# A relational graph layer on one core: five sweeps of neighbour sums instead of four, their groups spread evenly from unit 111

## The chip, the cores and the metric

The kernel runs on one core of a Trainium2 chip. The metric is device time in microseconds (us) of one execution; lower is better. TensorE is called PE here, VectorE DVE, ScalarE ACT, GpSimd POOL and SyncE SP.

## What is computed

```
h = relu(layernorm(x))                      # x: 1250 x 1024, fp32
u = h @ root + bias
for r in range(8):                          # 8 relations, 20000 edges, sorted by dst
    mask  = (edge_type == r)
    sums  = segment_sum(h[src] * mask, dst) # 1250 rows
    cnt   = segment_sum(mask, dst)
    u    += (sums / max(cnt, 1)) @ weight[r]
z   = concat([u, h]) @ w_gate + b_gate
out = x + tanh(u) * z + h * (1 - z)
```

All matrices are 1024 x 1024 in fp32, `w_gate` is 2048 x 1024.

## The kernel before

**Products.** The kernel multiplies first and sums afterwards: for each relation, y = h @ weight[r] goes to DRAM as two fp16 halves per value (`y_rows`, 4 KB a row), and the mean over a node's edges is taken of rows of y. PE's products run as eleven "gemms" in the order rel0, rel1, root, rel2 to rel7, gate_h, gate_u, cut into 325 **units**. A unit of the first three and of gate_u is 24 matmuls of 128 x 512; a unit of the other seven, which are done by a Winograd-like scheme of seven phases of five units, is 12 matmuls. `FIRST` gives each gemm's first unit: 0, 20, 40, 60, 95, 130, 165, 200, 235, 270, 305. Products go to four PSUM banks in turn, so PE may be four units ahead of what DVE and ACT have read out.

**Sums.** The edges are sorted into 80 **groups** (relation r, 125 destination rows j), each of some 250 edges, and a group's edges into **tiles** of 128, two or three a group. POOL prepares a tile: it copies its indices (L600), gathers 128 rows of y with an indirect DMA into a ring of four slots (L610; 4 KB a row), and makes a 128 x 125 one-hot matrix of the destinations (L618). It makes the one-hot of tile t-2 before it gathers tile t, so two gathers are in flight. PE multiplies one-hot and rows (L1243, four matmuls, and one for the counts, L1246) into PSUM banks 4 to 6. When the group's last tile is done, DVE divides by the counts and adds to the rows of u (L1111 to L1113, `add_group`). A tile's slot is free again when PE has done it; the next group's first tile waits for `add_group` of the group before, since banks 4 to 6 are the only ones.

**Sweeps.** u is too large to stay on chip, so the groups are walked in **sweeps** over the ten row blocks: sweep 0 has relations 0 to 2, sweep 1 has 3 and 4, sweep 2 has 5 and 6, sweep 3 has 7. In each, SP loads a block of 125 rows of u, the groups (j, r) of the sweep are added, and SP stores it again (L400, L409; three buffers). This is a **step**; a sweep has ten. A sweep's tiles are padded to a multiple of four; that gives 72, 48, 48 and 24 tiles with these edges, 192 in all. At a sweep's end POOL makes the last two one-hots, loads the next bounds, and waits until all rows of y of the next sweep's relations are stored (L635 to L646).

**Order.** All order is written by unit number. `AGG_AT[g]` is the unit behind which PE does the first tile of group g (`sum_first`), `REST_AT[g]` the unit behind which it does its other tiles (`sum_rest`). DVE does `add_group(g)` at the head of unit `REST_AT[g] + 1`. SP stores and loads a block of u two units after a step's last rest, ahead of that unit's y store in its queue. The list of edges is made on POOL with 160 indirect DMAs (L585) and comes back as a table, from which `table()` on DVE (L990 to L992) makes the indices at unit `TABLE_AT`, at the end of the unit's work.

In sweep 2 the first tile and the rest of a group stand at the same unit; in the other sweeps the rest is one unit later where the next group leaves room. The last groups, of rel7, are tied to the end of rel7's products (unit 269), and their results to gate_u, whose left operand is u.

Of the kernel before, what the change touches and what calls it, by code (L numbers as in the profile page):

```python
# [21 lines left out]
def gated_rgcn_preln(nc, x, src, dst, edge_type, weight, root, bias, w_gate, b_gate, out):  # L22
# [6 lines left out]
    NJ = N // DT  # L29
    NG = R * NJ  # L30
    RING = 4
    TMAX = 332
    HC = 512
    HT = 5
    KH = 4
# [2 lines left out]
    PAD = LT[NJ - 1][1]  # L38


    SWEEPS = [(0, 3), (3, 5), (5, 7), (7, 8)]
    NS = len(SWEEPS)
    SPAN = [(r0 * NJ, r1 * NJ) for r0, r1 in SWEEPS]
    assert EP * EC == E and NJ * DT == N and 2 * NG + E // P + NS * (RING - 1) <= TMAX - RING and TMAX % RING == 0
    assert len(LT) == NJ and D == 2 * KH * P and R == 8 and NJ == 2 * HT

    def group(g):

        for s, (a, b) in enumerate(SPAN):
            if g < b:  # L50
                r0, r1 = SWEEPS[s]
                j, r = divmod(g - a, r1 - r0)
                return s, j, r0 + r
# [60 lines left out]
    for n in range(NU):  # L114
# [4 lines left out]
        else:  # L119
# [2 lines left out]
            FREED.append((kind, tally[kind]))  # L122


    AGG_AT = ([98 + g * 67 // 30 for g in range(30)] + [168 + g * 68 // 20 for g in range(20)]
              + [238 + g * 34 // 20 for g in range(20)] + [273 + g * 28 // 10 for g in range(10)])
    assert all(AGG_AT[g] >= FIRST[W_OF[SWEEPS[group(g)[0]][1] - 1] + 1] + 3 for g in range(NG)) and AGG_AT == sorted(AGG_AT)

    REST_AT = [AGG_AT[g] + (1 if g + 1 < NG and AGG_AT[g + 1] >= AGG_AT[g] + 2 and group(g)[0] != 2 else 0) for g in range(NG)]
    AGG, REST = {}, {}  # L130
    for g in range(NG):
        AGG.setdefault(AGG_AT[g], []).append(g)
        REST.setdefault(REST_AT[g], []).append(g)
    STEPS = [(s, j) for s in range(NS) for j in range(NJ)]
    STEP_END = [REST_AT[SPAN[s][0] + (j + 1) * (SWEEPS[s][1] - SWEEPS[s][0]) - 1] for s, j in STEPS]
    FINAL = (NS - 1) * NJ
# [16 lines left out]
    SQ = 4  # L153
    KEYS_AT, SCAN_AT, TOTALS_AT, BOUNDS_AT = 2, {5: 0, 9: 1, 13: 2, 15: 3}, 17, 19
    POSITIONS_AT = {21: 0, 25: 1, 29: 2, 33: 3}
    TABLE_AT = AGG_AT[0] - 3
    NCONST = 5 + 2 * NS

    hs_rows = nc.dram_tensor("hs_rows", [N, D], F32).ap()
    y_rows = [nc.dram_tensor(f"y_rows{i}", [(r1 - r0) * N, 2 * D], F16).ap() for i, (r0, r1) in enumerate(SWEEPS)]  # L160
    table_rows = nc.dram_tensor("table_rows", [P * TMAX, 1], I32).ap()
    zh_rows = nc.dram_tensor("zh_rows", [N, D], F32).ap()
# [62 lines left out]
    with ctx:  # L225
        def sb(name, shape, dt):
            return ctx.enter_context(nc.sbuf_tensor(name, shape, dt))
# [9 lines left out]
        early = sb("early", [P, 8 * D], F32)  # L237
        edges = sb("edges", [P, TMAX, 2], I32)
        table_i = sb("table_i", [P, TMAX], I32)
        tb = sb("tb", [P, NG], F32)  # L240
# [118 lines left out]
        def _(sp):  # L359
# [73 lines left out]
            for n in range(NU):  # L433
# [35 lines left out]
                if n == FIRST[W_ROOT + 1] + 2:  # L469
                    sp.wait_ge(s[YDONE], 2 * NJ * (W_ROOT + 1))  # L470
                    load_brow(b_gate)
                if n == AGG_AT[0] - 2:
                    for b in range(4):
# [47 lines left out]
        def _(pool):  # L521
# [112 lines left out]
            for i in range(NS):  # L634
                q0 = pool.value_load(turns[0:1, i:i + 1], min_val=0, max_val=TMAX // RING - 2)  # L635
                q1 = pool.value_load(turns[0:1, i + 1:i + 2], min_val=0, max_val=TMAX // RING - 1)
                for b in range(4):
# [160 lines left out]
        def _(dve):  # L798
# [356 lines left out]
            for n in range(NU):  # L1155
# [28 lines left out]
                if n in POSITIONS_AT:  # L1184
                    positions(POSITIONS_AT[n])
                if n == TABLE_AT:
                    table()
# [13 lines left out]
        def _(pe):  # L1201
# [127 lines left out]
            for n in range(NU):  # L1329
# [12 lines left out]
                for g in range(NG):  # L1342
                    if AGG_AT[g] == n:
                        sum_first(g)
                    if REST_AT[g] == n:
                        sum_rest(g)
# [26 lines left out]
```

## Time and profile before

| | us |
|---|---|
| median of 3 runs | 1476.33 |
| lowest, highest | 1475.23, 1481.91 |
| the profiled execution | 1475.66 |
| its span in the trace | 1473.8 |
| PE busy in the span | 1294.7 (88%) |
| DVE busy | 938.9 (64%) |
| POOL busy | 728.8 (49%) |
| ACT busy | 409.2 (28%) |
| moved by DMA | 259.15 MB, 176 GB/s over the span |

The span is the time from the first to the last instruction of the trace. PE is the busiest engine but stands still for parts of the span. The products of the units are line L1285, those of the tiles L1243. Units can be found in the trace by counting: each is 12 (or 24) matmuls of L1285. A timeline row with "x60" is five units of 12.

### The profile page before, as it was taken

Reading aid. Unit: us, or ns where it says so; the run is one execution under the profiler, and the core shown is the slowest. Engines: PE = TensorE matmul, PEld = TensorE weight load, DVE = VectorE, ACT = ScalarE, POOL = GpSimd, SP = SyncE. Lnnn points to the kernel's source line nnn. Section 1 sums busy time; section 2 is a strip of 40 time slices with the busy share of each in tenths; the row PEclk is TensorE's granted clock in tenths of the full one; section 3 lists DMA queues with packets and bytes.
Section 4 is the critical chain, followed back from the end, with each engine's and each line's share of the span. In section 5 each row is a group of like instructions: output and inputs, shape, how many; then the busy total and the mean of one; then the engine's idle time right before and its main releaser. Section 6 shows DMA issues by size and latency. Waiting matters only on the chain.

```text
span 1473.8 us, 19899 instructions
## 1 busy us (share of the span) xinstructions
PE 1294.7 (88%) x6165; PEld 650.2 (44%) x6165; DVE 938.9 (64%) x1256; ACT 409.2 (28%) x501; POOL 728.8 (49%) x801
## 2 busy tenths in 40 slices
PE   3998999999998299899898999998977878878996
PEld 1444444444443144444444454444433434444663
DVE  6587688575664366565465667666534556686766
ACT  5443223122333022321132143243202213343000
POOL 2422078787878556565645547444555454420000
PEclk9998999999999599999999999999999999999998
DMA  5542143252244266867664866774776855856676
GB/s 210 196 158 83 40 132 87 53 164 59 57 117 132 76 204 220 265 193 233 200 194 145 271 216 182 255 233 153 227 233 207 253 169 172 272 182 190 177 223 200
DMA packets 108104, 259.15 MB, mean 176 GB/s; under 512 B 20826, under 2 KB 21329, under 8 KB 108020
## 3 DMA queue, kind: packets, MB, share of 16 engines
q1 hardware_dynamic: 75204, 175.63, 36.2%
q0 software_dynamic: 32816, 82.39, 19.9%
q8 instruction: 55, 0.90, 0.3%
q14 instruction: 29, 0.24, 0.1%
HBM read 194.34 MB, written 82.17 MB: 188 GB/s over the span
## 4 chain that ended last, share of the span: by engine, by line
PE 33%; POOL 19%; DMA 19%; DVE 13%; issue 11%; ACT 3%; SPq 2%; POOLq 1%; DVEq 0%; ACTq 0%
PE ps L1285 25%; POOL table_rows L585 16%; DMA early<-y_rows,pair 13%; PE ps L1243 6%; DMA out_dram<-hT 3%; DVE W L914 2%; SPq L418 1%; POOL onehot L618 1%; DMA hT<-zh_rows 1%; DVE early L1113 1%; DVE hT L962 1%; ACT early L703 1%; POOL pair L600 1%; DVE yhl L1036 1%; DVE urow L1120 1%
## 5 line engine op out<-in xcount | busy, mean ns | idle before, releaser
L1285 PE MATMUL ps<-W,hT 128*128 128x512 f16 (+2 forms) x4860 | 1102.3, 385 | 9.3 <-DVE W L914 7.0
L1285 PEld LDWEIGHTS ps<-W,hT 128*128 128x128 f16 (+2 forms) x4860 | 494.1, 104 | 553.7 <-issue 46.2
L610 POOL DMA_INDIRECT early<-y_rows,pair x192 | 231.2, 1204 | 149.4 <-PE ps L1246 101.6
L1243 PE MATMUL ps<-early,onehot 128*125 x768 | 205.9, 398 | 107.6 <-POOL onehot L618 81.4
L585 POOL DMA_INDIRECT table_rows<-edges,table_i x160 | 241.7, 1511 | 114.1 <-issue 57.2
L618 POOL TENSOR_SCALAR onehot<-iota_d,pair 128x125 f16<-128x125 f16 x184 | 153.6, 835 | 201.1 <-DMA early<-y_rows,pair 197.8
L743 ACT ACTIVATE yhl<-W 128x512 f16<-128x512 f32 x120 | 75.3, 628 | 396.5 <-DVE W L1036 207.4
L1243 PEld LDWEIGHTS ps<-early,onehot 128*125 x768 | 104.8, 141 | 178.9 <-issue 128.8
L914 DVE SCALAR_TENSOR_TENSOR W<-W,wsc 128x2048 f16<-128x2048 f32 x65 | 152.5, 2351 | 24.0 <-ACT W L693 24.0
L693 ACT ACTIVATE W<-W,wsc 128x2048 f16<-128x2048 f32 x65 | 128.3, 1990 | 74.2 <-DVE W L930 35.9
L660 ACT ACTIVATE peek_out<-W 128x1024 bf16<-128x1024 f32 x84 | 88.4, 1052 | 98.3 <-DMA W<-in_L_gnn_weight_dram 73.4
L1113 DVE SCALAR_TENSOR_TENSOR early<-ps,inv,early 125x1024 f32<-125x1024 f32 x80 | 102.7, 1284 | 2.8
L1001 DVE TENSOR_TENSOR yhl<-W,yhl 128x512 f16<-128x512 f32 x120 | 82.5, 687 | 1.4 <-ACT yhl L743 1.0
L1036 DVE SCALAR_TENSOR_TENSOR W<-ps,Q 128x512 f32<-128x512 f32 x60 | 41.3, 688 | 54.6 <-PE ps L1285 33.1
L1036 DVE SCALAR_TENSOR_TENSOR W<-ps,hT 128x512 f32<-128x512 f32 x60 | 41.3, 688 | 50.7 <-PE ps L1285 37.9
L600 POOL COPY pair<-edges 128x2 int32 x192 | 57.9, 301 | 27.8 <-DMA y_rows<-yhl 27.7
L1111 DVE TENSOR_SCALAR inv<-ps,wsc 125x1 f32<-125x1 f32 x80 | 17.1, 214 | 84.0 <-PE ps L1246 82.5
L930 DVE TENSOR_TENSOR W<-W 128x2048 f32<-128x2048 f32 x28 | 64.1, 2289 | 0.2
L1022 DVE SCALAR_TENSOR_TENSOR yhl<-ps,yhl 128x512 f16<-128x512 f32 (+1 forms) x40 | 26.8, 686 | 57.8 <-ACT yhl L735 57.6
L560 POOL TENSOR_TENSOR early<-early 128x1024 f16<-128x1024 f32 (+1 forms) x10 | 21.3, 2128 | 84.8 <-ACT early L708 84.8
L1036 DVE SCALAR_TENSOR_TENSOR Q<-ps,Q 128x512 f32<-128x512 f32 x60 | 41.1, 685 | 32.3 <-PE ps L1285 32.3
L735 ACT ACTIVATE yhl<-ps 128x512 f16<-128x512 f32 (+1 forms) x40 | 23.5, 594 | 103.7 <-PE ps L1285 99.5
(161 smaller groups left out, 676.1 us busy)
## 6 DMA issues: line engine op xcount, KB each, us to landing
y_rows<-yhl SPq DMA_DIRECT2D x144, 256.0 KB, 2.2
W<-in_L_gnn_weight_dram SPq DMA_DIRECT2D x32, 1024.0 KB, 6.9
early<-u_rows SPq DMA_DIRECT2D x40, 448.0 KB
u_rows<-early SPq DMA_DIRECT2D x40, 448.0 KB
W<-in_L_gnn_w_gate_dram SPq DMA_DIRECT2D x8, 1024.0 KB, 7.9
early<-in_x_dram SPq DMA_DIRECT2D x9, 512.0 KB, 4.4
hs_rows<-early SPq DMA_DIRECT2D x9, 512.0 KB, 2.9
u_rows<-yhl SPq DMA_DIRECT2D x18, 256.0 KB, 2.0
```

The source lines that it names most:

```text
L585: pool.indirect_dma_start(out=table_rows, out_offset=bass.IndirectOffsetOnAxis(ap=at_i[:, c:c + 1], axis=0), in_=packed[0:EP, c:c + 1], in ...
L610: pool.indirect_dma_start(out=G[:, b, :], out_offset=None, in_=y_rows[i], in_offset=bass.IndirectOffsetOnAxis(ap=idx[:, b, :], axis=0), bo ...
L618: pool.tensor_scalar(onehot[:, b, 0:DT], iota_d[:, :], dcol[:, b, :], None, ALU.is_equal).then_inc(s["tile_ready"], 1)
L660: nc.scalar.activation(peek_out[:, :], W[:, LAND[w][q], half * D:(half + 1) * D], ACT.Abs, accum_out=wsum[:, w, 2 * q + half:2 * q + half ...
L693: nc.scalar.activation(Wv[:, MAT[w][c], 0, :], W[:, at, :], ACT.Copy, scale=wscale(w, 0)).then_inc(s["w_hi"], 1)
L743: nc.scalar.activation(yhl[:, o % 4, 0, :], C[:, o % 4, :], ACT.Copy).then_inc(s["y_hi"], 1)
L914: nc.vector.scalar_tensor_tensor(out=Wv[:, MAT[w][c], 1, :], in0=W[:, at, :], scalar=wscale(w, 0), in1=Wv[:, MAT[w][c], 0, :], op0=ALU.mul ...
L1001: nc.vector.tensor_tensor(yhl[:, o % 4, 1, :], C[:, o % 4, :], yhl[:, o % 4, 0, :], ALU.subtract).then_inc(s[YDONE], 1)
L1036: return nc.vector.scalar_tensor_tensor(out=to, in0=part, scalar=scale, in1=of, op0=ALU.mult, op1=ALU.add)
L1113: nc.vector.scalar_tensor_tensor(out=ub[0:DT, b, :], in0=ps[0:DT, 4:6, :].rearrange("p b n -> p (b n)"), scalar=inv[0:DT, 1:2], in1=ub[0:D ...
L1243: nc.tensor.matmul(ps[0:DT, 4 + half, :], hot_t, rows[:, bass.ds(ring_slot * (2 * D) + (half * D + part * HC), HC)], start=first and part ...
L1285: last = nc.tensor.matmul(ps[0:rows, n % 4, :], hT[:, m, v_h, k, n0:n0 + rows], Wh[:, MAT[w][c], v_w, k, :], start=(first and v_h + v_w == ...
```

## The change

- `SWEEPS` has five entries: (0, 3), (3, 5), (5, 6), (6, 7), (7, 8). Relations 5 and 6 have a sweep each. There is one more DRAM tensor for y, ten more steps and so ten more loads and stores of a block of u. The tiles come to 72, 48, 24, 24 and 24, again 192.
- `AGG_AT` starts at unit 111 instead of 98. Sweep 0 takes units 111 to 173 (before 98 to 163), sweep 1 175 to 219 (before 168 to 233), sweep 2 222 to 244, sweep 3 246 to 271 (relations 5 and 6 were at 238 to 270). Rel7's groups stay at 273 to 299.
- `REST_AT` is one unit behind `AGG_AT` in every sweep, where the next group leaves room.
- `TABLE_AT` is `AGG_AT[0] - 4`: unit 107 instead of 95. SP's first two loads of u follow `AGG_AT[0]`, from unit 96 to 109.
- `TMAX`, the columns of the table, is 336 instead of 332. All lines behind L124 are one further down.

```
-    TMAX = 332
+    TMAX = 336
...
-    SWEEPS = [(0, 3), (3, 5), (5, 7), (7, 8)]
+    SWEEPS = [(0, 3), (3, 5), (5, 6), (6, 7), (7, 8)]
...
-    AGG_AT = ([98 + g * 67 // 30 for g in range(30)] + [168 + g * 68 // 20 for g in range(20)]
-              + [238 + g * 34 // 20 for g in range(20)] + [273 + g * 28 // 10 for g in range(10)])
+    AGG_AT = ([111 + g * 64 // 30 for g in range(30)] + [175 + g * 46 // 20 for g in range(20)]
+              + [222 + g * 24 // 10 for g in range(10)] + [246 + g * 27 // 10 for g in range(10)]
+              + [273 + g * 28 // 10 for g in range(10)])
...
-    REST_AT = [AGG_AT[g] + (1 if g + 1 < NG and AGG_AT[g + 1] >= AGG_AT[g] + 2 and group(g)[0] != 2 else 0) for g in range(NG)]
+    REST_AT = [AGG_AT[g] + (1 if g + 1 < NG and AGG_AT[g + 1] >= AGG_AT[g] + 2 else 0) for g in range(NG)]
...
-    TABLE_AT = AGG_AT[0] - 3
+    TABLE_AT = AGG_AT[0] - 4
```

**DVE around the table.** Before, at the head of rel3's units (95): L1036 and L1001 read out a product, L990 to L992 are `table()`, L930 and L914 prepare weights, L1109 begins the first `add_group`.

```order
L1036 SCALAR_TENSOR_TENSOR W<-ps,hT 128x512
L1001 TENSOR_TENSOR yhl<-W,yhl 128x512 x2
L990 TENSOR_SCALAR edges<-table_i 128x332
L991 TENSOR_SCALAR table_i<-table_i 128x332
L992 CAST edges<-table_i 128x332
L930 TENSOR_TENSOR W<-W 128x2048 x2
L914 SCALAR_TENSOR_TENSOR W<-W,wsc 128x2048
L930 TENSOR_TENSOR W<-W 128x2048
L1109 TENSOR_LOAD bounds
```

After, at unit 107 (L991 to L993 are `table()`, L1110 begins `add_group`):

```order
L1037 SCALAR_TENSOR_TENSOR Q<-ps,Q 128x512 x2
L991 TENSOR_SCALAR edges<-table_i 128x336
L992 TENSOR_SCALAR table_i<-table_i 128x336
L993 CAST edges<-table_i 128x336
L915 SCALAR_TENSOR_TENSOR W<-W,wsc 128x2048
L1037 SCALAR_TENSOR_TENSOR Q<-ps,Q 128x512 x2
L1037 SCALAR_TENSOR_TENSOR hT<-ps,Q 128x512 x3
L915 SCALAR_TENSOR_TENSOR W<-W,wsc 128x2048
L1110 TENSOR_LOAD bounds
```

Twelve units' read-outs, with the sums and halves of weights among them, now stand ahead of the three instructions of the table.

**PE at units 242 to 244.** Before: units 242 and 243 (x24), then a whole group (its first tile from L1250 to the first L1246, its rest in the loop that L1260 closes), then unit 244 and the next group at once.

```order
L1285 MATMUL ps<-W,hT 128x512 x24
L1250 TENSOR_LOAD bounds
...
L1246 MATMUL ps<-ones_h,onehot 125x2
L1258 TENSOR_LOAD bounds
...
L1260 COMPARE_AND_BRANCH
L1285 MATMUL ps<-W,hT 128x512 x12
L1250 TENSOR_LOAD bounds
```

After: unit 243, a first tile, unit 244, the rest, then units 245 and 246 and the first tile of the next group.

```order
L1286 MATMUL ps<-W,hT 128x512 x12
L1251 TENSOR_LOAD bounds
...
L1247 MATMUL ps<-ones_h,onehot 125x2
L1286 MATMUL ps<-W,hT 128x512 x12
L1259 TENSOR_LOAD bounds
...
L1261 COMPARE_AND_BRANCH
L1286 MATMUL ps<-W,hT 128x512 x24
L1251 TENSOR_LOAD bounds
```

Each rest has moved behind a unit of its own, and between two groups stand two or three units.

**SP behind the last weights of rel7 (unit 223).** Before: a step's store and load of u, in 112 and 13 rows, then seven stores of y until the next one.

```order
L375 DMA W<-in_L_gnn_weight_dram 128x4x512
...
L409 DMA u_rows<-early 112x1024
L409 DMA u_rows<-early 13x1024
L400 DMA early<-u_rows 112x1024
L400 DMA early<-u_rows 13x1024
L386 DMA y_rows<-yhl 128x1024 x6
L386 DMA y_rows<-yhl 98x1024
L409 DMA u_rows<-early 112x1024
```

After: two stores of y between steps.

```order
L376 DMA W<-in_L_gnn_weight_dram 128x4x512
...
L401 DMA early<-u_rows 112x1024
L401 DMA early<-u_rows 13x1024
L387 DMA y_rows<-yhl 128x1024 x2
L410 DMA u_rows<-early 112x1024
L410 DMA u_rows<-early 13x1024
L401 DMA early<-u_rows 112x1024
L401 DMA early<-u_rows 13x1024
L387 DMA y_rows<-yhl 128x1024 x2
L410 DMA u_rows<-early 112x1024
```

Four more DMAs of u now stand ahead of every second or third store of y.

## Rows read from the trace of the kernel before

**Rows 1.** Waits of PE: us in total, times, longest

```profile
PE ps L1243 <- POOL onehot L618: 81.4, 29, 31.8
```

**Rows 2.** Timeline of PE, sweep 0: start, duration, line, count

```profile
646.51 1.03 PE L1243 MATMUL ps<-early,onehot 128*125 x4
...
647.40 2.75 PE L1285 MATMUL ps<-W,hT 128*128 128x512 f16 x12
```

**Rows 3.** Timeline of PE around the first tile

```profile
461.67 13.11 PE L1285 MATMUL ps<-W,hT 128*128 128x512 f16 x60
506.57 1.94 PE L1243 MATMUL ps<-early,onehot 128*125 x4 [31.78 <-POOL onehot L618]
...
508.37 4.33 PE L1285 MATMUL ps<-W,hT 128*128 128x512 f16 x12
```

**Rows 4.** Timeline of DVE around the table

```profile
461.87 0.69 DVE L1036 SCALAR_TENSOR_TENSOR W<-ps,hT 128x512 f32<-128x512 f32 x1 [0.43 <-PE ps L1285]
...
493.49 0.33 DVE L990 TENSOR_SCALAR edges<-table_i 128x332 int32<-128x332 int32 x1 [25.71 <-DMA table_i<-table_rows]
```

**Rows 5.** Timeline of POOL: first gather and first one-hot

```profile
497.63 2.43 POOL L610 DMA_INDIRECT early<-y_rows,pair  x1 [0.70 <-POOL pair L600]
...
503.65 2.59 POOL L618 TENSOR_SCALAR onehot<-iota_d,pair 128x125 f16<-128x125 f16 x1 [2.22 <-DMA early<-y_rows,pair]
```

**Rows 6.** Windows of sweeps 0 to 2: us, busy of each engine, PE clock, DMA share, GB/s

```profile
508.40:773.40 265.00, 243.05 (x1142) 122.42 (x1141) 157.49 (x230) 70.15 (x90) 155.44 (x210) 0.97 0.69 216
783.60:1005.90 222.30, 216.70 (x1038) 107.83 (x1037) 145.72 (x202) 73.00 (x93) 117.07 (x145) 0.99 0.67 215
1016.10:1194.70 178.60, 144.70 (x640) 73.23 (x639) 91.14 (x134) 36.39 (x46) 101.85 (x145) 0.92 0.70 221
```

**Rows 7.** The same windows: products alone (first row), then tiles (L1246, one each)

```profile
508.40:773.40 265.00, 184.23 (x781) 73.62 (x782) 0.97 0.69 216
...
508.40:773.40 265.00, 12.13 (x72) 9.91 (x71) 0.97 0.69 216
...
1016.10:1194.70 178.60, 8.24 (x48) 7.22 (x48) 0.92 0.70 221
```

**Rows 8.** Waits of PE and POOL in sweep 2, 1016.1 to 1194.7

```profile
PE ps L1243 <- POOL onehot L618: 30.1, 21, 3.1
...
POOL onehot L618 <- DMA early<-y_rows,pair: 58.2, 29, 5.3
...
POOL early L610 <- PE ps L1246: 2.6, 1, 2.6
```

**Rows 9.** Waits of PE and POOL in sweep 0, 508.4 to 773.4

```profile
PE ps L1243 <- POOL onehot L618: 9.2, 5, 3.8
...
POOL early L610 <- PE ps L1246: 15.0, 10, 3.0
```

**Rows 10.** Timeline of POOL from sweep 2 to sweep 3

```profile
1186.73 1.07 POOL L610 DMA_INDIRECT early<-y_rows,pair  x1 [0.26 <-issue]
...
1192.00 0.59 POOL L646 TENSOR_SCALAR onehot<-iota_d,pair 128x125 f16<-128x125 f16 x1
1196.19 0.18 POOL L600 COPY pair<-edges 128x2 int32 x1 [3.60 <-DMA y_rows<-yhl]
```

**Rows 11.** DMA issues: count, KB each, median us to landing

```profile
early<-u_rows SPq DMA_DIRECT2D x40, 448.0 KB
...
early<-y_rows,pair POOLq DMA_INDIRECT x192, 5.2
```

**Rows 12.** DMA queues in sweep 2, 1016.1 to 1194.7: packets, MB, share

```profile
q0 software_dynamic: 6912, 20.77, 39.0%
q1 hardware_dynamic: 7689, 18.55, 30.7%
```

**Rows 13.** A window inside the last sweep, columns as in rows 6

```profile
1250.00:1275.00 25.00, 24.78 (x150) 13.44 (x149) 19.46 (x30) 9.07 (x9) 12.52 (x16) 1.00 0.84 286
```

**Rows 14.** Timeline of PE at the first tile of the last sweep

```profile
1207.58 1.62 PE L1243 MATMUL ps<-early,onehot 128*125 x4 [5.05 <-POOL onehot L618]
```

## The prediction

> **What bounds the kernel now.** I read the waits of all engines first, then the timeline around the start of the sums, then the windows of the sweeps, because a share of busy time alone doesn't tell which stage can give anything. In all waits, TensorE loses most to the one-hot matrix of a tile, 81.4 us in 29 waits [rows 1]. So TensorE (PE) sets the time, and what it lacks are gathered rows.
>
> The price of its own work comes from the undisturbed timeline [rows 2]: 12 products of a Winograd unit start 0.89 us after the tile before them began, and five units in a row take 13.11 us, where the first takes 2.75 [rows 2, 3]. (13.11 - 2.75) / 4 = **2.59 us a unit; 0.89 us a tile.**
>
> The start [rows 3 to 5]: the five units 94 to 98 begin at 461.67, so unit 98 begins at 472.0; then PE stands 31.78 us until tile 0. VectorE stands 25.71 us before the table arrives, in `table()`, which is in its queue ahead of unit 95's evacuation. POOL issues the first gather at 497.63.
>
> Then the sweeps [rows 6, 7]. A stretch is set against units x 2.59 + tiles x 0.89:
> - sweep 0, 508.4 to 773.4: 65 units (781 product records) and 72 tiles, 232 us of work in 265: 33 lost.
> - sweep 1, 783.6 to 1005.9: 66 units and 48 tiles, 214 in 222: 9 lost.
> - sweep 2, 1016.1 to 1194.7: 33 units and 48 tiles, 128 in 178.6: 50 lost. PE waits 21 times for one-hots, POOL 58.2 us for gathers to land and only 2.6 for PE [rows 8]: here the gathers are the bound, at 178.6 / 48 = **3.72 us a tile**.
>
> In sweep 0 POOL waits 15.0 us for PE, and PE 9.2 for POOL [rows 9]: neither is the bound alone. Its pace is 265 / 72 = 3.68 a tile, nearly that of sweep 2, though it has 3.2 us of PE work a tile and sweep 2 has 2.7.
>
> **The change, part by part.**
>
> *Start at unit 111 instead of 98.* `table()` moves on VectorE from behind unit 95 to behind unit 107. PE no longer stands still: unit 98 starts at 472.0 and 14 units (98 to 111) end at 472.0 + 36.3 = 508.3. Unit 107's product ends at 472.0 + 10 x 2.59 = 497.9; its evacuation takes 0.69 and the table's three instructions, 0.33 each with what lies between them, about 1.1 (before, from 493.49) [rows 4], so the table is ready at 499.7 instead of 494.6, and everything on POOL is 5.1 us later: one-hot 0 ends at 506.2 + 5.1 = 511.3 [rows 5]. PE waits some 3.4 us, does tile 0 in 1.9, and starts unit 112 at **513.4**. Before, unit 99 started at 508.37 [rows 3]. So 13 units (33.7 us) are gained and 5.0 given back. If VectorE were late at 107, each us of that would be one of PE's.
>
> *Sweep 0* now has 62 units (112 to 173) and the same 71 tiles behind tile 0: 160.6 + 63.2 = 223.8 us of work. With the 33 lost as before it takes 257; if the gathers set it, the 265 of before. I take 262, since POOL was waited for on both sides: unit 174 starts at **775.4**.
>
> *Sweep 1* spans units 174 to 221, 48 of them, with 48 tiles: 124.3 + 42.7 = 167.0 of work. Before, it had 18 units more and hid its gathers; now the gathers at 3.72 want 178.6. That is the cover which goes. I take 184: unit 222 at **959.4**.
>
> *Sweeps 2 and 3*, which were one, have 24 units and 24 tiles, then 27 and 24: 83.5 and 91.3 of work, 89.3 each by gathers at 3.72. The bursts of three tiles at one unit (order of PE, above) go. What is new is one more pass over u: ten loads and ten stores of 125 x 1024 fp32, 10.2 MB, on SP's queue. Before, 40 such loads [rows 11]. In the stretch of sweep 2 gathers moved 20.77 MB and the SP queue 18.55 MB [rows 12]; of the latter 10.2 are u, which leaves 8.3 for 33 units, 0.25 MB a unit. After: 20.8 + 20.5 + 51 x 0.25 = 54 MB in both. In 178.6 us this would be 302 GB/s; the highest 25 us window that I found with gathers in it has 286 at a share of 0.84 [rows 13]. So gathers should land later there; I take 4.0 and 4.2 us a tile, 96 and 101 us, or 274 GB/s: unit 273 at **1156.4**.
>
> The Trainium skill (DMA: Bandwidth & Descriptors, Measured) has a single core's large loads at up to 425 GB/s; by that, 302 would cost nothing and both sweeps would take 179 to 181 us, 16 less than I take. No run here shows such a rate over a sweep, and the window's share of 0.84 at 286 speaks against it.
>
> *A boundary between sweeps.* POOL lets its last two gathers land before it loads the next bounds: last gather at 1186.73, last one-hot at 1192.00 to 1192.59, next index copy at 1196.19, the last 3.6 us of that for y rows [rows 10]. Without this wait it should go on near 1194, where a steady stream would have issued at 1190.5: some 3.5 us each, and new code for the fifth sweep. Boundaries 0|1, 1|2 and 2|3 no longer wait for y, since their rows are stored long before. The two units of gap on PE cover it about; zero to 3.5 each, inside what I took.
>
> *SP's queue.* At each step end SP waits for `u_added`, stores, waits for the store of the step before, and loads, ahead of the unit's y store. With one relation a step, it does so every 2.4 units, not every 3.4. What is queued behind are y stores (four buffers, waited for by ACT and VectorE) and the weights. A step lasts about 9.5 us, more than a store takes by any row here, so I cost it at nothing beyond the bytes; if a store took longer than a step it would be worth some us each.
>
> *Small edits.* The fifth sweep adds four selects on POOL, one loop of edge keys and one bounds instruction on VectorE, and TMAX widens the table by 1.2%: below 1 us each, and the table's arrival now has 5 us in hand (493.49 against 498.6), so nothing. The later rest of sweep 2's groups is part of the even spread.
>
> *The tail.* Rel7's groups stay at 273 to 298, their first gather waits for the rows of unit 269 as before, and PE then waited 5.05 us [rows 14]. Unit 273 began at 1207.58 - 5.05 - 2.75 = 1199.8; from there to the end stay 274.0 us.
>
> **Sum:** 1156.4 + 274.0 = 1430.4 of span, 43.4 less; the profiled execution lay 1.9 above its span (1475.66 against 1473.8) and 0.7 below the median of the runs. 1430.4 + 1.9 + 0.7 = **1433.0 us**.
>
> **The rivals.**
>
> *A, the gathers follow.* If evenly spread tiles let PE lose as little as in sweep 1 (9 in 48 tiles) everywhere behind sweep 0: 770.6 + 167.0 + 83.5 + 91.3 + 18 = 1130.4 at unit 273, or 1407 us. For it: POOL waited 15 us for PE even in sweep 0, so its own pace can be (265 - 15) / 72 = 3.5. Against: sweep 2's 3.72 with POOL hardly ever waiting for PE.
>
> *B, DMA throughput is the bound (slower).* If the core's queues give no more than the 221 GB/s of sweep 2 [rows 6] while gathers run, sweep 1 (20.8 + 10.2 + 48 x 0.25 = 43 MB) takes 195 us and sweeps 2 and 3 (54 MB) 244: unit 273 at 775.4 + 195 + 244 = 1214, the end at 1491 us, 15 slower. It decides from 230 GB/s down: there 97 MB take 422 us, and 775.4 + 422 is 1197. For it: 215 to 221 GB/s in three sweeps [rows 6] whatever PE did. Against: windows of 286, and gathers that wait for their own landing with two in flight.
>
> *C, half of it.* Queues give 245 GB/s: 175 + 220 us, unit 273 at 1171 to 1175, the end at 1450; with boundaries uncovered, 1460.
>
> *D, the change doesn't do what it says*: VectorE is late at `table()` or PE stands elsewhere between 98 and 111, for instance for the halves of weights that DVE makes (L914). All of the first 28.7 us would be lost and the rest stays gather-bound: about 1462.
>
> **Chances.** Forecast 0.60; A 0.14; C 0.14; D 0.04; B and what lies near it 0.08. The range 1404 to 1462 takes in A's upper part and C, and leaves out the rest of A, and B. About 0.5% (7.4 us) is what a measurement of this kernel tells from no change: faster than 1469: 0.87; within: 0.07; slower: 0.06.
>
> **What would show it.** In the profile of the changed kernel: PE's wait of 31.8 us gone and one of 2 to 6 near 508; VectorE's wait of 25.7 before the table gone; sweep 0 again 255 to 265 us; behind it about 184 us to unit 222 with POOL waiting for gathers rather than for PE; sweeps 2 and 3 at 4.0 to 4.2 a tile and 260 to 280 GB/s, with gathers landing later than the median of 5.2 us of before [rows 11]; the stretch from unit 273 at 274. It would be wrong if sweeps 2 and 3 take over 230 us (B), or under 185 (A), or if the tail changes by more than 3 us.

## The result, and the profile after

The changed kernel takes 1460.38 us (median of 15 runs, 1452.13 to 1473.89); the kernel before took 1480.20 in the same comparison (15 runs, 1472.35 to 1488.14). The ratio is 0.989, 95% interval 0.986 to 0.992: 16 us faster by the ratio and 20 by the medians, where 43 were forecast.

The profiled execution of after took 1452.13 us, the shortest of its 15, and its span is 1450.4. Spans of the two profiles therefore differ by 23.4 us, more than the medians do.

| us | before | after | forecast |
|---|---|---|---|
| unit 98 starts | 472.0 | 474.1 | 472.0 |
| unit 112 | 557.7 | 520.3 | 513.4 |
| unit 174 | 810.7 | 776.5 | 775.4 |
| unit 222 | 964.0 | 970.3 | 959.4 |
| unit 246 | 1058.0 | 1068.6 | |
| unit 273 | 1199.8 | 1174.9 | 1156.4 |
| end | 1473.8 | 1450.4 | 1430.4 |

The starts are counted from the matmuls of the products, 12 or 24 a unit.

**The start.** PE's timeline at the first tile, against [rows 3]:

```profile
504.77 5.78 PE L1286 MATMUL ps<-W,hT 128*128 128x512 f16 x26
518.54 1.94 PE L1244 MATMUL ps<-early,onehot 128*125 x4 [7.99 <-POOL onehot L619]
```

The wait of 31.78 us has become one of 7.99. VectorE's timeline at the table, against [rows 4], shows that its wait went from 25.71 to 2.69, but that the table came at 503.61 instead of 493.49:

```profile
503.61 0.34 DVE L991 TENSOR_SCALAR edges<-table_i 128x336 int32<-128x336 int32 x1 [2.69 <-DMA table_i<-table_rows]
```

POOL's timeline, the last three scatters of edges, the first gather and the first one-hot; against [rows 5]:

```profile
488.89 3.07 POOL L586 DMA_INDIRECT table_rows<-edges,table_i  x1 [0.30 <-issue]
492.26 3.09 POOL L586 DMA_INDIRECT table_rows<-edges,table_i  x1 [0.30 <-issue]
497.70 1.19 POOL L586 DMA_INDIRECT table_rows<-edges,table_i  x1 [2.35 <-issue]
...
507.82 1.10 POOL L611 DMA_INDIRECT early<-y_rows,pair  x1 [0.71 <-POOL pair L601]
...
517.59 0.62 POOL L619 TENSOR_SCALAR onehot<-iota_d,pair 128x125 f16<-128x125 f16 x1 [7.30 <-DMA early<-y_rows,pair]
```

**The sweeps.** Windows of the four sweeps between units 112 and 273, columns as in [rows 6]:

```profile
520.30:776.50 256.20, 234.71 (x1104) 118.71 (x1103) 159.16 (x226) 68.35 (x89) 161.59 (x213) 0.97 0.69 216
776.50:970.30 193.80, 174.98 (x821) 87.16 (x820) 111.73 (x156) 44.71 (x56) 106.10 (x150) 0.97 0.73 231
970.30:1068.60 98.30, 86.80 (x412) 43.64 (x411) 64.44 (x90) 32.78 (x43) 57.23 (x74) 0.98 0.81 257
1068.60:1174.90 106.30, 95.13 (x448) 47.22 (x447) 65.27 (x96) 27.12 (x37) 55.10 (x74) 0.98 0.87 279
```

Against units and tiles at their undisturbed price, 2.59 and 0.89 us, 32.4, 26.8, 14.8 and 15.0 us are lost in them, 89 in all. DMA moves more per second from sweep to sweep, up to 279 GB/s at a share of 0.87.

What TensorE and POOL wait for over the whole span; the first row answers to [rows 1]:

```profile
PE ps L1244 <- POOL onehot L619: 46.1, 27, 8.0
PE ps L1244 <- DVE early L1114: 33.2, 19, 3.7
```

```profile
POOL onehot L619 <- DMA early<-y_rows,pair: 230.1, 123, 7.3
POOL early L611 <- PE ps L1247: 61.0, 19, 10.7
```

PE's wait for the add (L1114) is what the prediction did not price. Between 508 and 1200 us PE of before waited 15.2 us for the add of a group (9 times); PE of after waits 25.2 (16 times). The rest of its 33.2 lies in the last sweep, as before (23.9 in the whole span of before).

One such wait, at unit 188. VectorE's timeline first, then PE's:

```profile
834.19 2.35 DVE L915 SCALAR_TENSOR_TENSOR W<-W,wsc 128x2048 f16<-128x2048 f32 x1 [0.45 <-ACT W L694]
836.45 0.21 DVE L1112 TENSOR_SCALAR inv<-ps,wsc 125x1 f32<-125x1 f32 x1
...
836.90 1.28 DVE L1114 SCALAR_TENSOR_TENSOR early<-ps,inv,early 125x1024 f32<-125x1024 f32 x1
```

```profile
831.60 1.03 PE L1244 MATMUL ps<-early,onehot 128*125 x4
832.46 0.17 PE L1247 MATMUL ps<-ones_h,onehot 128*125 128x2 f16 x1
832.49 2.75 PE L1286 MATMUL ps<-W,hT 128*128 128x512 f16 x12
838.58 1.94 PE L1244 MATMUL ps<-early,onehot 128*125 x4 [3.35 <-DVE early L1114]
...
840.38 3.25 PE L1286 MATMUL ps<-W,hT 128*128 128x512 f16 x12
```

The group's sums are in PSUM at 832.6, but VectorE has 2.35 us of weights (L915) ahead of the add. PE, which needs banks 4 to 6 for the next group's first tile, stands 3.35 us. Then the tile takes 1.94 instead of 1.03 us and the next unit 3.25 instead of 2.75, so a stop costs more than its own length. The reason is TensorE's clock. Windows at the tile and inside the unit behind it (the clock is the third number from the end, as a share of 2.4 GHz):

```profile
838.60:840.40 1.80, 1.80 (x6) 1.04 (x7) 1.38 (x3) 0.63 (x1) 0.61 (x2) 0.50 0.55 139
841.50:843.50 2.00, 2.00 (x11) 0.95 (x10) 0.00 (x0) 0.00 (x0) 1.73 (x3) 1.00 0.95 270
```

While PE stood, the granted clock fell to half (1.2 GHz); it was back at full about 1 us into that unit. From the tile's start to the unit's start are 1.80 us at half clock and 0.89 at full.

### The profile page after: what moved, and what is told of

It reads as the page before. It is cut to its first block, busy times and chain, and to the rows that moved or that the text cites. A ratio compares the mean times of both kernels' runs of the same rounds, so it can differ in the third digit from the quotient of the medians.

```text
span 1450.4 us, 19965 instructions
## 1 busy us (share of the span) xinstructions
PE 1293.5 (89%) x6165; PEld 648.2 (45%) x6165; DVE 939.7 (65%) x1260; ACT 409.0 (28%) x501; POOL 734.0 (51%) x807
## 4 chain that ended last, share of the span: by engine, by line
DMA 26%; POOL 20%; PE 20%; issue 14%; DVE 13%; ACT 3%; SPq 2%; POOLq 1%; DVEq 0%; ACTq 0%
DMA early<-y_rows,pair 21%; POOL table_rows L586 17%; PE ps L1286 15%; PE ps L1244 4%; DMA out_dram<-hT 3%; DVE W L915 2%; SPq L419 1%; POOL onehot L619 1%; DVE early L1114 1%; POOL pair L601 1%; DMA hT<-zh_rows 1%; ACT early L704 1%; DVE hT L963 1%; DVE yhl L1037 1%; DVE urow L1121 1%
## 5 line engine op out<-in xcount | busy, mean ns | idle before, releaser
L586 POOL DMA_INDIRECT table_rows<-edges,table_i x160 | 249.9, 1562 | 114.3 <-issue 114.3
L1244 PE MATMUL ps<-early,onehot 128*125 x768 | 202.9, 391 | 84.1 <-POOL onehot L619 46.1
L915 DVE SCALAR_TENSOR_TENSOR W<-W,wsc 128x2048 f16<-128x2048 f32 x65 | 152.4, 2348 | 23.9 <-ACT W L694 23.7
L661 ACT ACTIVATE peek_out<-W 128x1024 bf16<-128x1024 f32 x84 | 88.4, 1052 | 93.9 <-DMA W<-in_L_gnn_weight_dram 71.3
L1114 DVE SCALAR_TENSOR_TENSOR early<-ps,inv,early 125x1024 f32<-125x1024 f32 x80 | 102.7, 1284 | 2.8
L1037 DVE SCALAR_TENSOR_TENSOR W<-ps,Q 128x512 f32<-128x512 f32 x60 | 41.4, 690 | 64.2 <-issue 37.4
L1002 DVE TENSOR_TENSOR yhl<-W,yhl 128x512 f16<-128x512 f32 x120 | 82.0, 684 | 1.3 <-ACT yhl L744 1.0
L1037 DVE SCALAR_TENSOR_TENSOR W<-ps,hT 128x512 f32<-128x512 f32 x60 | 41.3, 688 | 55.4 <-PE ps L1286 35.7
L1037 DVE SCALAR_TENSOR_TENSOR Q<-ps,Q 128x512 f32<-128x512 f32 x60 | 41.0, 685 | 38.3 <-PE ps L1286 38.3
L931 DVE TENSOR_TENSOR W<-W 128x2048 f32<-128x2048 f32 x28 | 64.1, 2291 | 0.1
L1023 DVE SCALAR_TENSOR_TENSOR yhl<-ps,yhl 128x512 f16<-128x512 f32 (+1 forms) x40 | 26.8, 686 | 57.4 <-ACT yhl L736 57.2
L1037 DVE SCALAR_TENSOR_TENSOR hT<-ps,Q 128x512 f32<-128x512 f32 x30 | 20.7, 690 | 63.3 <-PE ps L1286 63.3
```

Of the source, the lines that this page charges most:

```text
L586: pool.indirect_dma_start(out=table_rows, out_offset=bass.IndirectOffsetOnAxis(ap=at_i[:, c:c + 1], axis=0), in_=packed[0:EP, c:c + 1], in ...
L661: nc.scalar.activation(peek_out[:, :], W[:, LAND[w][q], half * D:(half + 1) * D], ACT.Abs, accum_out=wsum[:, w, 2 * q + half:2 * q + half ...
L915: nc.vector.scalar_tensor_tensor(out=Wv[:, MAT[w][c], 1, :], in0=W[:, at, :], scalar=wscale(w, 0), in1=Wv[:, MAT[w][c], 0, :], op0=ALU.mul ...
L1002: nc.vector.tensor_tensor(yhl[:, o % 4, 1, :], C[:, o % 4, :], yhl[:, o % 4, 0, :], ALU.subtract).then_inc(s[YDONE], 1)
L1037: return nc.vector.scalar_tensor_tensor(out=to, in0=part, scalar=scale, in1=of, op0=ALU.mult, op1=ALU.add)
L1114: nc.vector.scalar_tensor_tensor(out=ub[0:DT, b, :], in0=ps[0:DT, 4:6, :].rearrange("p b n -> p (b n)"), scalar=inv[0:DT, 1:2], in1=ub[0:D ...
```

## The experiments

All edits are against the changed kernel, unless one says otherwise. Ratios are to the kernel before, measured in the same comparison, with their 95% intervals.

### Round 1: which part gives what

**Four sweeps, late start.** Sums from unit 111, the table at 107, but relations 5 and 6 in one sweep. In that sweep first tile and rest of a group stand at one unit, as before.

```
-    SWEEPS = [(0, 3), (3, 5), (5, 6), (6, 7), (7, 8)]
+    SWEEPS = [(0, 3), (3, 5), (5, 7), (7, 8)]
...
+    AGG_AT = ([111 + g * 64 // 30 for g in range(30)] + [175 + g * 61 // 20 for g in range(20)]
+              + [238 + g * 34 // 20 for g in range(20)] + [273 + g * 28 // 10 for g in range(10)])
```

> The kernel before with one part of the change: four sweeps as they were, sweep 0 from unit 111 (64 units for its 30 groups), sweep 1 from 175 with 61 units, sweep 2 still at 238 to 270, the table at unit 107. Theory S (the gain comes from the start, and the fifth sweep gives little on top): sweep 1 keeps 58 units of cover, unit 238 comes 19 us earlier than before (1016 to about 997), the rest is as before: 1457 to 1463 us, as the changed kernel. Theory F (the even spread of sweeps 2 and 3 gives the gain, and what the start gives is lost again): 1470 to 1480 us.

1450.56 us, ratio 0.982 (0.978 to 0.986).

**Five sweeps, early start.** `AGG_AT` begins with `98 + g * 67 // 30` and `168 + g * 53 // 20`, the table at 95.

> The changed kernel with the start undone: five sweeps, the last four as changed from unit 222 on, but sweep 0 from unit 98 (67 units) and sweep 1 from 168 with 53 units; the table at unit 95. Theory S: 1470 us or more. Theory F: unit 222 at about 984, sweeps 2 and 3 in 205 us as in the changed kernel, unit 273 at 1189: 11 us below the kernel before, 1462 to 1469 us. In both, the last scatter of the table should start near 488, as in the kernel before, if it is VectorE's standing still that lets POOL's scatters run through (1.19 us each beside an idle VectorE, up to 4.9 beside a busy one), and near 498 if it was chance.

1470.96 us, 0.994 (0.991 to 0.997). The wait of PE at the first tile is back, 30.3 us long.

So the late start alone gives 27 us (medians 1477.14 and 1450.56), the fifth sweep alone 6 (1477.14 and 1470.96), and both together 13 to 24 in three comparisons, by medians: the two gains do not add up.

**Three gathers in flight.** One-hot t-3 is made before gather t; the ring of four slots stays. The first turn of a sweep is shown; its other turns and its end are changed alike.

```
-                for b in range(2, RING):
-                    make_onehot(i, q, b - 2)
+                gather(i, q, 2)
+                for b in range(3, RING):
+                    make_onehot(i, q, b - 3)
```

> The changed kernel with three gathers in flight instead of two: POOL makes the one-hot of tile t-3 before it gathers tile t. Bytes, tiles and order on PE are the same. Theory L (the landing time of a gather with two in flight sets the pace, 3.6 to 4.4 us a tile, and it rises with the load of the queues): the landing time rises, but the pace comes near PE's work: sweeps 0 to 3 take about 245, 178, 92 and 100 us instead of 256, 194, 98 and 106, unit 273 near 1137, 1418 to 1432 us. Theory T (what the DMA queues can move sets the pace, 231 to 279 GB/s): landing takes half again as long and the pace stays: within 7 us of the changed kernel.

1452.06 us, 0.981 (0.978 to 0.985). POOL's wait for landing falls from 230 to 31 us. What it waits for instead is PE (first two rows), and PE's waits have hardly changed (last two rows):

```profile
POOL onehot L619 <- DMA early<-y_rows,pair: 30.7, 22, 6.5
POOL early L611 <- PE ps L1248: 166.8, 67, 12.4
```

```profile
PE ps L1245 <- POOL onehot L619: 42.3, 29, 8.5
PE ps L1245 <- DVE early L1115: 39.7, 18, 3.6
```

The landing of gathers was a bound, but taking it away uncovers the next ones, the add and the slots: it gives only 5 to 12 us against the medians of after in three comparisons (1456.55 to 1463.72; ratios 0.984 to 0.990).

**The fifth pass over u with few bytes.** Stores of sweep 2 and loads of sweep 3 move 13 rows of a block instead of 112: of the other rows the sums are not carried on. In `load_u` and `store_u`:

```
+                    rows = 13 if sweep == 3 else rows
...
+                    rows = 13 if sweep == 2 else rows
```

> The changed kernel with the bytes of the added pass left out: in sweep 2 the store of a block of u and in sweep 3 its load move 13 rows twice instead of 112 and 13, with the same number of DMAs, waits and order (so u misses most rows of relation 5's sum and those before it). It takes 8.8 MB or so out of the 54 in sweeps 2 and 3. Theories L and T: the two sweeps fall from 205 to 185 to 192 us, in all 12 to 20 us below the changed kernel. Theory P (stalls of PE with VectorE and POOL, whatever the bytes): within 4 us of the changed kernel.

1454.27 us, 0.983 (0.980 to 0.987). Sweep 3's window, against after's 106.3 us at a share of 0.87:

```profile
1089.80:1184.20 94.40, 92.28 (x448) 46.46 (x447) 63.29 (x94) 25.72 (x36) 48.79 (x67) 1.00 0.78 250
```

Sweep 3 runs nearly without a stop, 12 us shorter than in the first profile of after and 5 than in the second; a gather lands in 5.2 us (median) there instead of 7.5. Sweep 2 takes 99.8 us, no less than after's 98.3. As a whole the kernel is 2 to 9 us faster than after by the medians, and the ratio's interval overlaps all of after's three: in this kernel the gain is not clear of the noise.

### Round 2: the late table, and the add

**The changed kernel once more**, and a third time in a later round, so that stages can be told from their spread.

> The changed kernel once more, beside the others on this chip and with a second trace. Its profiled execution so far was the shortest of its 15, 8 us under their median, while that of the kernel before was 4 us under its own. Expected: 1455 to 1466 us; if sweeps 1, 2 and 3 now take 203 to 215 us for the last two and over 190 for the first, the stages of the first trace are typical, and their excess over the forecast is no accident.

> The changed kernel beside these on the same chip, with a third trace: 1455 to 1463 us; units 112 to 273 in 655 to 662 us as in the first two traces.

1456.55 us, 0.984 (0.980 to 0.987), and 1463.72, 0.990 (0.987 to 0.994). From unit 112 to 273 the three profiles take 654.6, 660.7 and 664.3 us, so a stage in one profile is good to some 5 us. By stage, beside the forecast:

| us | first | second | third | forecast |
|---|---|---|---|---|
| sweep 0 | 256.2 | 261.8 | 261.0 | 262 |
| sweep 1 | 193.8 | 196.3 | 199.3 | 184 |
| sweeps 2 and 3 | 204.6 | 202.6 | 204.0 | 197 |
| from unit 273 | 275.5 | 272.5 | 279.3 | 274.0 |

**Groups moved off the units where PE stood for the add**: 18 groups of sweeps 0 to 3 (the expectation counts 21) by one unit or two, in sweep 1 for instance:

```
-[175 + g * 46 // 20 for g in range(20)]
+[175, 177, 179, 181, 184, 186, 188, 190, 192, 194, 196, 199, 202, 205, 207, 210, 212, 214, 216, 218]
```

> The changed kernel with 21 of its first 70 groups moved by one or two units, so that fewer rests stand at a unit at whose end VectorE has 2.3 us of weight work (halves or sums of quadrants) ahead of its add of the group. Spread, bytes and sweeps are the same. Theory P (VectorE's late adds make PE's stalls of 2 to 3.5 us at units 188, 195, 209, 224 and 243, which the trace of the changed kernel and that with three gathers in flight have in common): PE's waits for the add fall from 25 us to under 13 and the time by 5 to 12 us below the changed kernel. Theory L (the landing of gathers alone): within 4 us of it.

1459.71 us, 0.985 (0.980 to 0.990). PE waits for the add 32.2 us in 16 waits, hardly less than after's 33.2. In sweep 0 they fell from 12.3 to 7.6, and in sweep 2 they rose from 3.1 to 10.5: the stops have moved to other units.

```profile
PE ps L1246 <- DVE early L1116: 32.2, 16, 4.8
```

**Four sweeps with three gathers in flight.**

> Four sweeps with the late start (1450.6 us) and three gathers in flight. In the dense sweep 2 (238 to 270) tiles come in bursts and POOL waited 58 us for landings. Theory L: that stretch falls from 178 to 160 us or less, sweep 0 by some 5: 1425 to 1435 us. Theory T (moved bytes per us are the limit in the dense sweep): within 6 us of the late start alone.

1450.10 us, 0.979 (0.975 to 0.983): nothing clear against the 0.982 of four sweeps with two.

**The table read at unit 95, sums still from 111.** VectorE then stands still while POOL issues its last scatters.

```
-    TABLE_AT = AGG_AT[0] - 4
+    TABLE_AT = 95
```

> The changed kernel with the table back at unit 95 on VectorE, which then stands still from about 469 until the table is there, while PE stops at the fourth unit ahead of it. If VectorE's own work is what stretches POOL's scatters, the last scatter starts at 487 to 490 as in the kernels that start at 98, though the sums here start at 111; if it doesn't, at 495 to 498. PE loses about 22 us before unit 111, and 11 of the 13 units gained: unit 112 starts near 528 instead of 520.

1462.80 us (one run); PE stands as VectorE does, so the time says little. What it tells are the scatters. POOL's busy time in the scatters between 467 and 494 us, of before, of after and of this kernel:

```profile
467.00:494.00 27.00, 16.57 (x14) 0.69 0.27 62
467.00:494.00 27.00, 23.34 (x13) 1.00 0.19 48
467.00:494.00 27.00, 17.46 (x15) 0.91 0.14 25
```

VectorE stands still there in the first and third kernel and works in the second. One scatter takes 1.2 us in the first and third, and 1.8 in the second; the two in POOL's timeline above with 3.07 and 3.09 lie beside weight work of VectorE:

```profile
488.54 2.35 DVE L915 SCALAR_TENSOR_TENSOR W<-W,wsc 128x2048 f16<-128x2048 f32 x1
...
492.00 2.29 DVE L931 TENSOR_TENSOR W<-W 128x2048 f32<-128x2048 f32 x1
```

The first ran from 488.54 to 490.89, and the scatter beside it, begun at 488.89, ended at 491.96, 1.07 us behind that; the second ended at 494.29, and its scatter at 495.35, 1.06 behind. Over the whole chain of after 51 of 160 scatters take more than 1.3 us (44 before), and nearly all of them end 1.06 us behind the VectorE instruction that ran when they began; these are sums and scalings of two operands in SBUF (L915, L931, L1002, L977). The 12 scatters that began beside L1037, which reads one of its two operands from PSUM, kept their 1.19 us. So a scatter waits for the whole instruction and then does its work. The last scatter starts at 487.6, 497.7 and 488.7 us in the three.

### Round 3: the add ahead of the weights

**The add at the unit's head.** `add_group(g)` moves from the head of the next unit, behind the weight work, to ahead of it, one unit earlier.

```
-                for g in REST.get(n - 1, ()):
-                    add_group(g)
...
+                    for g in REST.get(n, ()):
+                        add_group(g)
```

> The changed kernel with VectorE's add of a group moved from the head of the unit behind the rest to the end of the rest's own unit, ahead of that unit's weight work (2.3 us halves and sums), which comes later by the time VectorE waits for the group's last tile. Theory P: PE's waits for the add (33 us in 19, stalls of 2 to 3.5 us) fall under 10 us, and with the clock that they cost the time falls by 15 to 25 us from the changed kernel. Theory L: PE then waits for one-hots instead, since gathers at 3.7 us or more a tile are the bound: at most 5 us. A third way: weights come late and PE waits for L915: slower.

1463.73 us, 0.988 (0.985 to 0.991): no gain against after's 0.984 to 0.990. The waits for the add fall from 33.2 to 11.9 us, and those for one-hots rise from 46.1 to 63.9:

```profile
PE ps L1244 <- POOL onehot L619: 63.9, 31, 5.8
...
PE ps L1244 <- DVE early L1114: 11.9, 8, 3.6
```

**The same with four sweeps**, with two and with three gathers in flight.

> Four sweeps with the late start (1450 us) and the add ahead of the weight work. Theory P: PE's waits for the add in sweep 0 (10.5 us) and the last sweep go, 8 to 15 us faster than the late start alone: 1436 to 1442. Theory L: within 4 us.

> The same with three gathers in flight. If both bounds stand one behind the other (the add, then the landing), the two edits together bring more than the sum of each alone (about 0 for three in flight): 1420 to 1432 us. If the tiles' pace is set by the four slots of the ring, which PE frees, nothing is added: within 4 us of the add alone.

1455.18 us, 0.983 (0.978 to 0.987), and 1445.63, 0.976 (0.973 to 0.980).

**The same with five sweeps and three gathers in flight.**

> Five sweeps, add ahead of the weight work, three gathers in flight. If the bytes of the fifth pass over u are what costs (landing 7.1 us in sweep 3 against 5.6), three in flight should hide them and this comes level with the four sweeps under the same two edits; if not, it stays 6 to 12 us above.

1433.59 us, 0.968 (0.965 to 0.971). Alone, three in flight gave 5 to 12 us and the earlier add nothing; together they give 23 to 30, and 30 against the earlier add alone in the same comparison. In all four kernels with the earlier add, units 273 to 305 take 164.5 to 168.5 us, where after takes 156.4 to 162.1 in three profiles: in the last sweep it costs time.

### Round 4: both, but not in the last sweep

```
+                for g in REST.get(n - 1, ()):
+                    if g >= SPAN[NS - 1][0]:
+                        add_group(g)
...
+                    for g in REST.get(n, ()):
+                        if g < SPAN[NS - 1][0]:
+                            add_group(g)
```

> Five sweeps, three gathers in flight, the add ahead of the weight work in sweeps 0 to 3 only (in the last sweep, where the earlier add came with 166 instead of 156 us from unit 273 to 305, it stays where it was). If that last stretch was lengthened by the earlier add: 1422 to 1428 us, 5 to 11 below the 1433.6 with the add ahead everywhere. If it was chance: 1430 to 1437.

> The same two edits with four sweeps and the late start. It tells what the fifth sweep alone is worth once landing and add are no longer bounds: by the two kernels with the add ahead everywhere (1445.6 against 1433.6) the five sweeps should be 8 to 14 us faster than these four, whereas without the two edits they were 6 to 10 us slower. Expected 1433 to 1441.

> The first kernel of this call without most bytes of the added pass over u (in sweep 2's stores and sweep 3's loads 13 rows twice instead of 112 and 13, so u misses most of the sums before). If bytes set what is left in sweeps 2 and 3 (96 and 102 us against 83.5 and 91.3 of PE's work): 8 to 15 us faster than with them. If it is the coupling of PE, POOL and VectorE over four slots: within 4 us.

With five sweeps 1427.07 us (1421.20 to 1429.76), ratio **0.966** (0.962 to 0.971), 3.4% faster than before and the best of all. With four 1436.19, 0.973 (0.968 to 0.977). With five and the light fifth pass (the same rows left out as above) 1417.15, 0.960 (0.956 to 0.964). VectorE's timeline of the best kernel where after had its stop at unit 188, and what its PE waits for in all:

```profile
825.63 1.28 DVE L1115 SCALAR_TENSOR_TENSOR early<-ps,inv,early 125x1024 f32<-125x1024 f32 x1
826.83 2.34 DVE L916 SCALAR_TENSOR_TENSOR W<-W,wsc 128x2048 f16<-128x2048 f32 x1
```

```profile
PE ps L1249 <- POOL onehot L619: 45.9, 31, 8.2
PE ps L1249 <- DVE early L1115: 18.1, 12, 3.6
```

The add now stands ahead of the weights. The stretch from unit 112 to 273, in profiles:

| us, 112 to 273 | two in flight | three in flight |
|---|---|---|
| five sweeps, add behind weights | 654.6, 660.7, 664.3 | 647.9 |
| five sweeps, add ahead | 666.0 | 633.6, 626.7 |
| four sweeps, add behind weights | 659.6 | 654.9 |
| four sweeps, add ahead | 648.8 | 644.1, 641.6 |

Where the 28 us between after (654.6) and the best kernel (626.7) went can be added up. Both have 565.6 us of units and tiles there. PE's waits are those that the profile lists, and the time at half clock is that of its clock records; half of the latter, as an estimate, is what it cost:

| us, 112 to 273 | waits of PE | at half clock | waits + half of that | all that is lost |
|---|---|---|---|---|
| after | 62.8 | 31.0 | 78.3 | 89.0 |
| after, third profile | 66.2 | 44.4 | 88.4 | 98.7 |
| three in flight | 59.8 | 26.9 | 73.3 | 82.3 |
| add ahead | 65.8 | 48.2 | 89.9 | 100.4 |
| both, not in the last sweep | 43.7 | 14.5 | 51.0 | 61.1 |

Between 9 and 11 us stay over in every row, and what they are is open. Of the 28 us, 19 are waits and, by this estimate, 8 are clock: fewer stops also mean less time at half speed.

## Why the prediction was right in sign and wrong in size

Forecast and profile of after differ by 20.0 us of span (1430.4 and 1450.4): +6.9 at unit 112, -5.8 in sweep 0, +9.8 in sweep 1, +7.6 in sweeps 2 and 3, +1.5 behind unit 273. A further 7 us lie between profile and median: the profile of after stood 8.3 below its own median, where the forecast had added 0.7.

**The start: right in kind, 6.9 us off.** PE no longer stands between units 98 and 111, VectorE is not late, and rival D falls. The failed step is "the table's arrival now has 5 us in hand". It took the scatters from a row in which VectorE stood still, and the change itself sets VectorE to work there. The last scatter starts 10.1 us later (497.70 for 487.61; 1.7 of them were there at the chain's first scatter, 191.6 for 189.9; in the second profile it starts at 495.5). 5.1 were in hand, so the table comes 5.0 later than forecast. With VectorE put to rest again the last scatter starts at 488.7. That a scatter stretches beside VectorE is shown by the three kernels; which instructions do it was read from neighbours in time, not tried singly. The Trainium skill (SBUF — State Buffer, Who interferes with whom) has the rule: a VectorE instruction with two inputs in SBUF and a GpSimd instruction that reads SBUF lock each other out for the whole instruction. The trace agrees, with its 1.06 us behind each end. It speaks against the step, and I had not weighed it. The same section of the Trainium skill reports a probe in which `tensor_tensor` did not stall a DMA, and infers that it leaves free the port which the making of descriptors needs; here the scatter beside L931, a TENSOR_TENSOR, took 3.09 us for 1.19, and the measurement decides. The other 2 us lie between the table and the first tile, 14.9 us (503.61 to 518.54) where before had 13.1 (493.49 to 506.57): the first rows landed later, a wait of 7.30 us for 2.22 [rows 5]. This was not taken apart. One reading of the start was wrong without effect: before, unit 95's product is read out by ScalarE (L739, at 467.05), so VectorE's wait in `table()` held up later units only.

**Sweep 0** takes 256.2, 261.8 and 261.0 us in the three profiles, for 262. It loses 32 to 38 us against the price of its work, where before lost 33. So this term was right within the spread.

**Sweep 1** is the largest miss, 193.8 us for 184, and 196.3 and 199.3 in the other two profiles. The step that failed is "what lacks are gathered rows", with 3.72 us a tile as the only other price. Gathers at that price allow 178.6. What came on top is the add: 8.8 us in 5 waits there, beside 7.7 in 5 for one-hots, and 10.2 us at half clock, which cost about 5.

```profile
PE ps L1244 <- DVE early L1114: 8.8, 5, 3.3
PE ps L1244 <- POOL onehot L619: 7.7, 5, 2.8
```

Both bounds stand in one loop: a gather waits for a slot, a slot for PE, PE for the add, and the add for weight work. Before, a sweep with 66 units for 48 tiles left room for either; with 48 units it doesn't. [rows 9] showed both directions of waiting in sweep 0, and I read them as a reason to take a value between two prices instead of as a sign of a chain. The same view of before had a longer wait of PE in sweep 0, which I left out:

```profile
PE ps L1243 <- DVE early L1113: 12.7, 7, 2.6
```

In sweep 1 before, this wait came to 0.4 us. The change gave sweep 1 the spacing of sweep 0, about two units a group, and with it such waits. The runs show the chain: each bound taken away alone gives 5 to 12 us or none, both give 30 (1433.59 against 1463.73 with the earlier add alone) and 37 (1427.07 against 1463.72 of after in the same comparison). In sweep 1 itself three in flight take 188.0 us, the earlier add 195.6, and both 184.8 and 180.2. The forecast's size is reached only by these two kernels (1427 and 1434 us, against 1433), with two edits that the forecast did not have, so that is no point in its favour.

**Sweeps 2 and 3** take 98.3 and 106.3 us for 96 and 101 (204.6, 202.6 and 204.0 together in the three profiles), at 257 and 279 GB/s, 268 over both, near the forecast of 274. Gathers land later as forecast: median 6.2 and 7.5 us against 5.2. So rival B falls, since no rate of 221 or 230 holds the queues. The Trainium skill (DMA: Bandwidth & Descriptors, Measured) allows more by its 425 GB/s, but a gather's landing already rises by 2 us at 279 here, so with a fixed number in flight the bytes cost time long before that rate. The term was 6 to 8 us short.

**The bytes of the fifth pass** cost 10 us in the best kernel (1417.15 for 1427.07, without overlap of their runs); in the changed one the 2 to 9 us are not clear of the noise. Rival C had the right end (unit 273 at 1171 to 1175, the kernel at 1450 to 1460) by luck. It gave sweep 1 175 us and the two sweeps behind it 220, where 194 and 205 were measured, and its 245 GB/s are not a limit, since 257 and 279 were moved. Its reason is right only in part: bytes slow the landing of gathers, but the largest miss is in sweep 1, whose bytes had not grown.

**Rival A** falls: even the shortest run took 45 us more than its 1407, with 89 us lost instead of 33 + 18. (Its sum begins with 770.6, where its terms give 770.2.)

**The even spread and the fifth sweep** were to give what the late start alone couldn't. They don't in this kernel: four sweeps with the late start are at 0.982 (0.978 to 0.986), the change at 0.984 to 0.990 in three comparisons, so the fifth sweep costs between nothing and some 12 us. Where it costs is open: from unit 112 to 273 four sweeps take 659.6 us and five 654.6 to 664.3, and the difference in the profiles stands behind 273 (150.0 us to unit 305 for 156.4 to 162.1), in which the two kernels have the same groups. The four sweeps with three gathers in flight take 158.5 there, so the 150.0 may be chance. With both bounds gone, five sweeps beat four by 9 us (1427.07 and 1436.19, intervals 0.962 to 0.971 and 0.968 to 0.977), 15 in the stretch. With the late start, five sweeps paid only when neither landing nor the add held the loop; with the early start they gave 6 us even so.

**The tail** is 275.5, 272.5 and 279.3 us in the three profiles, for 274.0; the third is beyond the 3 us that the prediction allowed it.

**Still open.** Even the best kernel takes 626.7 us where units and tiles come to 565.6; its PE waits 45.9 us for one-hots in all. What more slots in the ring, or a second set of PSUM banks for the sums, would give was not tried, though POOL waits 166.8 us for slots with three in flight. Of the 1.5% between runs of the changed kernel (1452 to 1474) the rows show a companion, not a first cause: the mean granted clock is 0.969 to 0.972 in the four shortest of its 15 runs and 0.961 to 0.966 in the four longest. Whether one-hots and gathers lose time beside VectorE as the scatters do (a one-hot takes 0.62 us at the start and 0.83 in the mean) was not tried.

## What to carry to other kernels

Two waits of like size in one loop of engines can act as one bound: price a change at each, and expect little from mending one of them alone; mend both in one kernel before you judge either. Read the list of waits of the stage in question to its end, since the wait that looks small over the whole kernel can be the largest there. Where a change fills an engine's idle time, take the durations of its neighbours from a stretch in which that engine worked, not from the idle one. What an engine does last before it frees a buffer belongs ahead of its long work that nobody waits for.

## What the runs showed of the hardware

- POOL's issue of an indirect scatter takes 1.19 us with VectorE at rest and up to 3.3 beside a 128x2048 instruction of VectorE with two operands in SBUF, whose end it waits for; beside one with an operand in PSUM (L1037) it stays at 1.19. Thirteen scatters between 467 and 494 us took 1.8 on average for 1.2, and the chain's end moved by 8 to 10 us.
- A gather of 128 rows of 4 KB took 5.2 us (median) from issue to landing at 250 GB/s, 6.2 at 257 and 7.5 at 279 (share 0.78, 0.81 and 0.87). In the second profile of after it took 5.3 at 252 and 7.1 at 291.
- TensorE's granted clock fell to half while PE stood 3.35 us, and was back at full within the next unit: the tile behind the stop took 1.94 us instead of 1.03, and the unit 3.25 instead of 2.75. From unit 112 to 273 after ran 31.0 us at half clock, and the best kernel 14.5.
